# Latent scores and contexts as 64x64 tiles of the array over two PSUM banks, weights in 2+2 quarters, own latent buffers in the last pass, the flag read inside the block

## What is computed

```python
# 1: 8 heads of 128 against a memory of 256 rows, three times over
Q = layernorm(hidden, g_state, b_state) @ Wq.T
for _ in range(NUM_STEPS):                                  # 3
    scores = jnp.einsum('bhsd,hnd->bhsn', xi, K) * beta
    w = entmax15(scores)
    xi = jnp.einsum('bhsn,hnd->bhsd', w, V)
out = xi.transpose(0, 2, 1, 3).reshape(B, S, H * hd) @ Wo.T
...
# 2: 16 heads of 64 against the 64 context rows of the same batch entry
scores = jnp.einsum('bhsr,bhlr->bhsl', q_r, k_r)
attn = jax.nn.softmax(scores, axis=-1)
ctx_c = jnp.einsum('bhsl,bld->bhsd', attn, kv_rope)
ctx_lat = jnp.einsum('bhsd,hkd->bshk', ctx_c, w_kc_kv)
out = ctx_lat.reshape(b, s, H * K) @ Wo.T
...
# 3: a dense layer
w = weight * scale_weight[:, None]
out = jnp.einsum('bsi,oi->bso', x, w) + bias
...
x = _layernorm(x + _L0_attn_ref(...)); x = _layernorm(x + _L0_xattn_ref(...)); x = _layernorm(x + _L0_ffn_ref(...))
```

## Time and profile before

| | us |
|---|---|
| median of 3 runs | 906.58 (906.13 to 909.62) |
| the profiled execution's own time | 906.48 |
| its span, first to last instruction | 904.6 |
| PE busy | 834.2 (92%) |
| DVE busy | 794.6 (88%) |
| ACT busy | 705.6 (78%) |
| POOL busy | 494.3 (55%) |

### The profile page before, as it was taken

One profiled execution on the slowest core, in us unless ns is written; L12 is line 12 of the kernel. 1 busy time (PEld: TensorE's weight loads), 2 busy tenths in 40 slices (PEclk: granted clock), 3 DMA queues, 4 the chain that ended last, 5 costly groups with the idle time before them and its releaser, 6 DMA issues.

```text
span 904.6 us, 17069 instructions
## 1 busy us (share of the span) xinstructions
PE 834.2 (92%) x4958; PEld 719.5 (80%) x4958; DVE 794.6 (88%) x2051; ACT 705.6 (78%) x1691; POOL 494.3 (55%) x2306
## 2 busy tenths in 40 slices
PE   6999996899999999999999999999999997999961
PEld 5877785688888888888888888888888886887850
DVE  3699999999999999999999999999998998978431
ACT  3588897998888989878989697989697789866320
POOL 4133536664564656666656566575645557654423
PEclk9999999999999999999999999999999998999995
DMA  8900020000000000000000001000000000000000
GB/s 280 204 1 1 16 91 11 9 2 2 1 1 1 1 1 13 1 3 1 1 1 1 12 2 30 7 1 1 2 1 19 1 1 7 7 1 7 7 1 27
DMA packets 24212, 17.55 MB, mean 19 GB/s; under 512 B 11761, under 2 KB 23537, under 8 KB 23857
## 3 DMA queue, kind: packets, MB, share of 16 engines
q1 hardware_dynamic: 23872, 16.13, 6.3%
q0 software_dynamic: 240, 0.27, 0.2%
HBM read 14.30 MB, written 2.10 MB: 18 GB/s over the span
## 4 chain that ended last, share of the span: by engine, by line
PE 65%; DVE 18%; ACT 7%; POOL 5%; issue 3%; DMA 1%; SPq 0%; POOLq 0%
PE banks L1227 24%; PE banks L1250 11%; DVE moments L793 7%; PE banks L1238 6%; PE banks L1278 6%; PE banks L1311 4%; PE banks L1101 4%; DVE top L773 4%; ACT work L704 3%; PE banks L1287 3%; DVE work L813 2%; PE banks L1303 2%; ACT work L695 1%; ACT work L716 1%; PE banks L1324 1%
## 5 line engine op out<-in xcount | busy, mean ns | idle before, releaser
L793 DVE BATCH_NORM_STATS2 moments<-work 128x6 f32<-128x512 f32 x576 | 373.7, 686 | 5.8 <-ACT work L704 2.9
L704 ACT ACTIVATE work<-work,neg_u 128x256 f32<-128x256 f32 x768 | 329.1, 519 | 47.5 <-DVE neg_u L805 25.6
L1227 PE MATMUL banks<-weights_s,work 128*128 128x256 f32 x1536 | 350.7, 381 | 6.1 <-ACT work L695 4.2
L1227 PEld LDWEIGHTS banks<-weights_s,work 128*128 128x128 f32 x1536 | 286.9, 191 | 46.2 <-issue 7.6
L695 ACT ACTIVATE work<-banks,neg_low 128x256 f32<-128x256 f32 x384 | 152.7, 494 | 10.2 <-DVE neg_low L784 10.0
L923 POOL TENSOR_TENSOR resid_sum<-moments 128x8 f32<-128x8 f32 x144 | 30.7, 214 | 226.6 <-DVE moments L793 225.4
L773 DVE MAX8 top<-banks 128x8 f32<-128x256 f32 x384 | 141.7, 415 | 8.2 <-PE banks L1227 7.4
L716 ACT ACTIVATE work<-banks 128x512 f32<-128x512 f32 x192 | 112.9, 611 | 24.4 <-PE banks L1238 23.9
L1238 PE MATMUL banks<-ident,work 128*128 128x128 f32 x768 | 107.9, 276 | 15.0 <-DVE work L813 7.5
L1250 PE MATMUL banks<-weights_s,work 128*128 128x256 f32 x512 | 115.0, 380 | 0.3 <-ACT work L716 0.3
L1238 PEld LDWEIGHTS banks<-ident,work 128*128 128x128 f32 x768 | 86.2, 141 | 31.9 <-DVE work L813 16.1
(11 more groups left out here) (155 smaller groups left out, 1154.2 us busy)
## 6 DMA issues: line engine op xcount, KB each, us to landing
work<-in_L_xattn_Wo_dram SPq DMA_DIRECT2D x2, 1024.0 KB, 11.0
out_dram<-work SPq DMA_DIRECT2D x16, 128.0 KB, 1.7
work<-in_L_xattn_w_kc_q_dram SPq DMA_DIRECT2D x2, 768.0 KB, 5.5
rows<-in_L_xattn_Wq_dram SPq DMA_DIRECT2D x1, 1536.0 KB, 13.8
rows<-in_x_dram SPq DMA_DIRECT2D x1, 1536.0 KB, 7.1
work<-in_L_attn_Wq_dram SPq DMA_DIRECT2D x1, 1024.0 KB, 10.3
work<-in_L_attn_Wo_dram SPq DMA_DIRECT2D x1, 1024.0 KB, 13.6
work<-in_ctx_dram SPq DMA_DIRECT2D x32, 32.0 KB, 2.2
```

The lines of the kernel that those rows point to most:

```text
L704: ins = nc.scalar.activation(q_resid[:, j, h, :], q_resid0[:, j, h, :], ACT.Relu, bias=small["neg_u"][:, j, h:h + 1])
L793: ins = nc.vector.bn_stats(moments[:, j, 2 * q:2 * q + 2, :].rearrange("p h k -> p (h k)"), r.rearrange("p h n -> p n h"))
L1227: ins = nc.tensor.matmul(ps_scores[:, h, :], lhsT, w[:, h, t, :], start=(t == 0), stop=(t == CT - 1))
```

## The change

Five things change.

- **`scores_lat` and `contexts`** use 64 rows by 64 columns of the array at a time. Head 0 of a pair (`odd` = 0) sits in rows 0 to 63, head 1 in rows 64 to 127, and only the 64x64 blocks that are not zero are used. Row halves write different banks: bank 6 + odd. `scores_lat` becomes one stage of 32 matmuls with 64 moving columns (before: two stages of 8 matmuls with 128), `contexts` one stage of 8 matmuls with 256 moving columns (before: two stages of 2 with 256, on all 128x128). In both, consecutive matmuls name different 64x64 tiles in the order (0,0), (1,1), (0,1), (1,0). Both stages hold banks 6 and 7 together, and wait for both halves of what is ahead of them. `latent_head` gives a new order of heads, used where the weights are prepared, so that `contexts` may put its output where `project_lat` reads it. `shift` reads its eight heads out of both banks.
- **Weights 2+2**: DVE makes quarters 0 and 1, ACT quarters 2 and 3 (`act_weights`).
- **Last pass**: tiles c to f have latent buffers of their own, in the area of their own `q_resid0`.
- **The flag** is awaited and loaded by each engine in the first block; the second block, the clearing of semaphores and the barriers around it are gone (they are done only if the general path is taken). SP waits for the stores after its load of the flag.
- **The turns** are new strings on all five engines.

The general path is rewritten in the same way in its contexts; it doesn't run.

```diff
+DVE_WEIGHTS = 2
+def latent_head(at):
+    chunk, side = at // 2, at % 2
+    return 2 * chunk + 8 * side if chunk < PAIRS // 2 else 2 * chunk - 7 + 8 * side
...
-        dve += four("weights", s)[:3]
-        act += once("last_weights", s) + four("square_weights", s)
+        dve += four("weights", s)[:DVE_WEIGHTS]
+        act += four("act_weights", s)[DVE_WEIGHTS:] + four("square_weights", s)
...
-    pe += four("project") + once("turn_x") + two("queries") + two("scores_lat") + two("turn_probs") + two("contexts")
+    pe += four("project") + once("turn_x") + two("queries") + once("scores_lat") + two("turn_probs") + once("contexts")
...
-        "SP": "3015249876304ac2db157f6e89abdecf",
+        "SP": "041236753280bc15a9fd74e986adbcef",
...
-        q_lat_q_t = q_probs_t = carve(work, 27328, PAIRS, P)
-        q_probs, q_lat_c_t = carve(work, 28352, XH, XD), carve(work, 28352, PAIRS, P)
+        def latent_places(p, j):
+            at = 27328 if p < PASSES - 1 else 2048 * j
+            q_lat_q_t = q_probs_t = carve(work, at, PAIRS, P)
+            return q_lat_q_t, carve(work, at + 1024, XH, XD), q_probs_t, carve(work, at + 1024, PAIRS, P)
...
+        def pq_scores(q):
+            return banks[:, 6:8, 256 * q:256 * (q + 1)].rearrange("p r (g l) -> p g r l", l=XD)
...
-                        nc.vector.tensor_reduce(q_nmax[:, j, heads], pq_scores[:, heads, :], AX_X, ALU.max,
+                        nc.vector.tensor_reduce(nmax, pq_scores(q), AX_X, ALU.max,
...
+                    if stage in ("scores_lat", "contexts"):
+                        return (6, 7)
...
-                        if q == 0:
-                            use = last(lambda what: what[0] in ("queries", "project_lat"))
-                            assert use is None or use[2][0] == "project_lat"
...
-                        pe.wait_ge(lat_emptied[j], emptied(p, "queries", q))
-                        bank_free(last, 6 + q)
-                        for g in range(4 * q, 4 * q + 4):
-                            for b in range(2):
-                                at = slice(64 * b, 64 * (b + 1))
-                                ins = nc.tensor.matmul(pq_scores[at, 2 * g:2 * g + 2, :], q_lat_q_t[:, g, at],
-                                                       q_kv_diag_t[:, j, b, :], start=True, stop=True)
+                        pe.wait_ge(lat_emptied[j], emptied(p, "queries", 1))
+                        for bank in (6, 7):
+                            bank_free(last, bank)
+                        for g in range(PAIRS):
+                            for odd, b in ((0, 0), (1, 1), (0, 1), (1, 0)):
+                                head, at = (slice(64 * n, 64 * (n + 1)) for n in (odd, b))
+                                ins = nc.tensor.matmul(banks[at, 6 + odd, XD * g:XD * (g + 1)], q_lat_q_t[head, g, at],
+                                                       q_kv_diag_t[head, j, b, head], start=True, stop=True)
...
-                        pairs = slice(4 * q, 4 * q + 4)
                         for b in range(2):
                             at = slice(64 * b, 64 * (b + 1))
-                            ins = nc.tensor.matmul(pq_pairs[:, pairs, at], q_kv_diag[:, j, b, :], q_probs_t[:, pairs, at],
-                                                   start=True, stop=True)
+                            for odd, side in ((0, 0), (1, 1), (0, 1), (1, 0)):
+                                head, to = (slice(64 * n, 64 * (n + 1)) for n in (odd, side))
+                                ins = nc.tensor.matmul(pq_pairs[to, 4 * odd:4 * odd + 4, at], q_kv_diag[head, j, b, head],
+                                                       q_probs_t[head, 4 * side:4 * side + 4, at], start=True, stop=True)
...
             @block.tensor
             def _(pe):
                 asked = pe.alloc_register("general_asked")
+                pe.wait_ge(flag_step, 4)
                 pe.reg_load(asked, flag[0:1, 0:1])
...
-        nc.clear_and_free_semaphores(one_pass_sems)
-        nc.all_engine_barrier()
-        with nc.Block() as block:
-            general_path(block, **GENERAL)
```

More of the change, by code:

```diff
@@ L515, in one_pass @@
             POOL_AT, POOL_PASS = (2, 12, 23), 37
-            MADE, MADE_PASS = {"turn_x": 1, "queries": 2, "scores_lat": 4, "turn_probs": 6, "contexts": 8, "project_lat": 10,
-                               "turn_dense": 11, "dense": 12}, 12
+            MADE, MADE_PASS = {"turn_x": 1, "queries": 2, "scores_lat": 4, "turn_probs": 5, "contexts": 7, "project_lat": 8,
+                               "turn_dense": 9, "dense": 10}, 10
             EMPTIED, EMPTIED_PASS = {"turn_x": 2, "queries": 3, "turn_probs": 5, "contexts": 7, "turn_dense": 9}, 9
@@ L670, in _ @@
                 of("SP").play(run)
-                for j in range(SLOTS):
-                    sp.wait_ge(stored[j], 16 * PASSES)
             @block.scalar
@@ L706, in run @@
                         ins.then_inc(resid_ready[j], 1)
-                    elif stage == "last_weights":
+                    elif stage == "act_weights":
                         act.wait_ge(u_ready[j], eval_count(p, s, EVALS - 1))
-                        for h in (6, 7):
+                        for h in pair:
                             ins = nc.scalar.activation(q_resid[:, j, h, :], q_resid0[:, j, h, :], ACT.Relu,
@@ L1091, in bank_free @@
                         elif stage in READ:
-                            pe.wait_ge(lat_read[j], read(p, stage, q if stage == "scores_lat" else 0))
+                            pe.wait_ge(lat_read[j], read(p, stage, 1 if stage == "scores_lat" else 0))
                         else:
-                            pe.wait_ge(lat_emptied[j], emptied(p, stage, q))
+                            pe.wait_ge(lat_emptied[j], emptied(p, stage, bank - 6 if stage == "contexts" else q))
                 def prep_job(x, last):
@@ L1327, in _, with general_path @@
                 of("PE").play(run)
-        def general_path(block, evals, first, slots):
+        def general_path(evals, first, slots):
             passes = TILES // slots
```

256 lines of the change are left out of this document (153 added, 103 removed).

## The result

The changed kernel takes 892.15 us (median of 4 runs, 890.66 to 893.01), the kernel before 907.25 beside it (906.13 to 909.62): a ratio of 0.9828, with a 95% interval of 0.9803 to 0.9854. That is 15.1 us less. The forecast was 881 (868 to 897), 25.6 less: the direction is right and the time lies inside the range, but the gain is 10 us smaller than forecast.

What follows compares the result with a forecast made beforehand. It took PE (98%) and DVE (95%) as full in the middle, ACT at 86%, and the tail as a chain. Terms -3 - 13.5 - 6 + 0.9 - 4.0 = -25.6 against 906.5 gave 881 us, range 868 to 897.

Steps and rivals of the forecast that it cites:

- The tiles: Latent scores and contexts: four 64x64 tiles run at once, 1.71 us less per tile, 27 us less PE work in all.
- B: Latent scores and contexts: row halves don't overlap, so PE's work stays; 901 us, chance 0.06.
- C: Latent scores: small pieces limited by issue at 59 ns each, so slower; 917 us, chance 0.05.
- The weights: Weights of the third quarter, moved from DVE to ACT: 30.0 us less on DVE, 43.6 us more on ACT.
- The front, 45 to 200 us: Stretch before latent work: DVE, ACT and PE nearly level, so 152 us taken, 3 us gained.
- The middle, 200 to 700 us: Main stretch: PE's work of 469 us at 96.5% busy takes 486.5 us, 13.5 us gained.
- The clock: All three stretches: TensorE at its 2.4 GHz level almost throughout, 0.98 to 1.00; no term in the sum.
- Rival A: Mostly the middle: PE gets its 27 us but ACT is waited for; 12 us gained, 894 us, chance 0.15.
- The last stretch: 700 to 871 us: 9 us gained at PE's old busy share, 6 taken because of the chain.
- The end of the last tile: After 871 us: POOL's chain keeps its list, but f's scores start it later, 0.9 us more.
- The flag: End of the span: flag loaded without the second block, 4.0 us less; 3.1 if it came as late as before.
- Moves that I had put at nothing: New order of heads and own latent buffers: nothing; shift out of two banks: no change.

## Why the prediction was right, and where it was off

*The tiles.* Right. 64 pieces of scores in 1.09 us and 16 of contexts in 1.09, "about 1.1" both. Rivals B and C, the row halves one after the other and the pace of issue, are excluded; the pace is 17 ns a piece, far below the 43 at which C decides. The Trainium skill (TensorE: Matmul & The Clock Gate, Wait — 56ns, not 53.3ns?) has starts never closer than about 25 ns, by which 64 pieces would take an estimated 1.6 us. The trace doesn't agree.

*The weights.* Right for the groups: DVE's fell from 90.0 to 62.1 us, ACT's grew from 43.6 to 86.0. What counts for the engines was smaller, 24 and 33 us, for the overlap named above.

*The front, 45 to 200 us.* Forecast 3 less, measured 0: the same 384 pieces of the entmax scores are done at 200 us. Part of it is the clock: PE had 10.2 us at the 1.2 GHz level here, busy for 7.1, and before 3.4, all busy. As half the time would do at full clock, the lower level cost PE about 2 us more than before (an estimate). That the three level engines waited for each other more than I had said is not shown.

*The middle, 200 to 700 us.* **This is the term that was mis-sized: 13.5 us forecast, none measured** between 200 and 660. I put PE's work at 469 us and took 96.5% as its busy share. The share came true (96.0%) and the work did not: in those 460 us PE was busy for 440.2, where 449.4 less the relief is 430.8. Of the 18.6 us relief in those 460 us 9.3 went into longer busy times of the same work, about half of them by the lower clock, and 9.3 into waiting. The clock was a term that I had left at nothing. A busy share near full in a trace was read as if PE set the pace alone; the prices (0.56 and 0.55) and the run with half the latent work (4.8 us for 26) say that it shares it with DVE.

Rival A (half of the gain, 894) has the right size, but not the signs that it named: PE's share did not fall to 94%, and ACT reached 91%, not 92 or above. PE does wait for ACT more. But it does so as much in the new order with the weights 3+1 and full rows (16.2 us in the 460) as in the changed kernel (15.6), so in this order ACT's added work is not the cause.

*The last stretch.* Forecast 6 less 0.9, measured 10.6 (from 660 us on). The 0.9 came true: from the start of f's queries to the last normalise 10.9 us became 11.7. The likely ground for the rest is that few tiles are in flight here and the latent stages are on the chain of each. `scores` and `project` have 2048 pieces together. From the start of the one with which nine tenths are done to that of the last the kernel before takes 111 us (741.0 to 852.2), the changed one 103 (738.4 to 841.1), the new order with full rows 108 and the old order with half the latent work 111. So part is the tiles' and part is the order's. The order's part is near what the clock gives: the kernel before has 6.8 us at the 1.2 GHz level in this stretch (750.4 to 757.3), PE busy for 6.2 of them, and the new order has none there, with either work.

*The end of the last tile.* Forecast 24 to 26 us from the last normalise to the end of the last norm, measured 25.0. *The flag.* Forecast 4.0, measured 4.1 in the trace of the changed kernel; alone in the kernel before it was 2.4 by the medians and 2.8 by the traces (8.2 to 5.4), so part of the 4.1 needs the new end around it. The prediction had named that part: with a flag as late as before it gave 3.1, and in the kernel with the flag alone it is as late as before.

*Moves that I had put at nothing.* "The new order" was treated as neutral but for a small share. It isn't: 23 us worse with the old work and 16 better with the new. The profile of before shows neither sign; the forecast should have kept its price open on both sides.

*Luck.* By the profiles the time lies inside the range because two errors cancel in part. Front and middle gave 16.5 us less than forecast, the last stretch 5.5 more. Without the latter it would be at 897.7, just outside.

What stays open is which places of the new order make it fit the new work. PE's waits for ACT ahead of the turned weights grew in every kernel with the new order (3.8 to 11.5 us in the changed one) and in the old order with 2+2, so they alone don't tell the two apart. One place where the new order loses can be named. In all eight kernels that have it PE waits for L709 or the weights near 320 to 335 us and the clock falls there to the 1.2 GHz level; in none of the six with the old order does it fall between 200 and 735 us. No kernel with this place mended was run.

## What to carry to other kernels

Where an order is written out by hand over several engines, an edit need not have a price of its own: measure it in the order that it will live in, and expect that an order made for the new durations may lose with the old ones, by 23 us here. To see whether a pipeline has become faster, count a stage that the change left alone up to a fixed time, in both traces; busy shares can stay or fall as forecast while nothing has moved. Look at the granted clock of the same stretches too: a wait that an order moves to another place can take the clock down there. To learn what a us of an engine is worth, add a known amount to it, and take as the amount what its busy time grew by and not the sum of the new group: here 11 us for a group of 20 on DVE. A price well below one says that the engine does not bound the kernel alone, and it holds for that place only.

## What the runs showed of the hardware

Four 64x64 tiles of the array, two row halves and two column halves, work at once in fp32: 64 weight loads and matmuls in 1.09 us, 17 ns each. Over full rows the same products took 2.01 us in the new form and 1.90 in the old.

The granted clock fell near 323 us, as shown above, after PE had waited, and near 165 us too (stretch, length, busy by engine, clock):

```profile
160.00:165.00 5.00, 1.76 (x11) 1.16 (x9) 4.96 (x15) 5.00 (x14) 3.97 (x18) 1.00 0.09 21
165.00:170.00 5.00, 1.75 (x11) 1.55 (x12) 3.90 (x10) 5.00 (x14) 3.81 (x22) 0.62 0.00 0
170.00:175.00 5.00, 5.00 (x19) 4.23 (x18) 4.66 (x11) 5.00 (x13) 2.28 (x13) 0.69 0.00 0
175.00:180.00 5.00, 4.99 (x29) 4.17 (x28) 4.59 (x15) 4.75 (x13) 3.89 (x18) 1.00 0.00 0
```

PE was busy for 1.8 us of each of the first two stretches; the second and the third have 0.62 and 0.69, a mixture of the 2.4 and the 1.2 GHz level, and the fourth is full again. In 170 to 175 PE was busy all the time and did 19 pieces where the next 5 us have 29. The clock over the whole run was 0.981 before and 0.975 in the changed kernel and in the old order with half the latent work, but also 0.976 in the new order with full rows: that less work on PE lowers it isn't shown.

The reduction over partitions on GpSimd takes 0.38 us of work and has 13.2 us of issue around it (5.83 and 7.36; before, 5.72 and 7.51), which nothing in the trace accounts for and which is gone when PE and DVE do the reduction.
